# Local attention: when the next batch's first queries are turned, and in which order VectorE works around them

## The chip, the cores and the metric

The kernel is one program on one core of a Trainium2 chip. The metric is the device time of one execution in microseconds (us). A core has five engines with an instruction queue each, which run side by side and wait for each other by semaphores: TensorE (PE: matmuls, with PEld for the loading of its weights), VectorE (DVE), ScalarE (ACT), GpSimd (POOL) and SyncE (SP), which here only starts transfers. An engine does its instructions strictly in the order in which they were written.

## The reference

The program is a decoder of two layers on 16 batches of 128 tokens with 256 features: a recurrent mixer, a grouped cross attention and a mixture of experts, then local (windowed) attention, another cross attention and a gated feed-forward stage. The change touches the local attention alone:

```python
q = rms_norm(x @ Wq.T, qn_w)     # 16 heads of 128
k = rms_norm(x @ Wk.T, kn_w)     # 4 heads of 128
v = x @ Wv.T                     # 4 heads of 128
q = q * cos + rotate_half(q) * sin
k = k * cos + rotate_half(k) * sin
scores = q @ k.T / sqrt(128)     # 4 query heads share a key head
scores = where((0 <= i - j) & (i - j <= 64), scores, min)
out = softmax(scores) @ v
x = x + out @ Wo.T
```

Its input is the layer norm of x.

## The kernel before

`windowed` does the local attention. The 16 batches t follow each other (`pairs`: two written out, a loop over pairs of batches, two written out). A batch has four steps g = 0 to 3, one for each key head with its four query heads. The work is pipelined over steps: in step g of batch t each engine also does the projections and rotations that later steps need (`ahead`) and the end of the step before (`earlier`). The order on each engine is written out by hand in its own function `one`; semaphores join them. What the names mean:

- `project` (PE, L2086): six 128x512 matmuls give one group of four query heads (q0 to q3), the keys k or the values v. ACT copies the result to `wi_raw` (L2181) and squares it (L2184).
- `rotate` (DVE): the sum of squares (L2288, `wi_sums`), the cosine product (L2303, `wi_straight`) and two half-wide sine products (L2305, `wi_crossed`). `join` (POOL, L1984) adds the two; for k it also multiplies by the scale (L1987). `find_scale` (POOL, L1972 and L1973) makes the scale from the sums.
- `turn_heads` (PE, L2050): four 128x128 transposes of a joined group. `take_turned` (ACT, L2200) copies them from PSUM to `wi_q_t` or `wi_k_t`.
- `scores` (PE, L2096 the mask, L2099 the products), `maximum` (DVE, L2310, `wi_top`), `shift` (DVE, L2319, `wi_bias`), `weigh` (ACT, L2209, four exponentials), `invert` (DVE, L2332), `normalise` (POOL, L1994, `wi_weights`), `turn_weights` (PE, L2064), `take_weights` (DVE, L2326, `wi_weights_t`), `attend` (PE, L2108), `take_attended` (ACT, L2216), `split_out` (DVE, L2273), `project_out` (PE, L2121).

Below, "weights of step g" are the softmax weights. The order of PE in a step is: projections of q or k, the scores of the step, projection of v, `turn_weights` of the step before, `project_out` of two steps before, `attend` of the step before, then the transposes for the next step. At the end of step 3 these are the keys k and the queries q0 of the next batch. POOL's order in step 2 is: scale of k, `normalise` of step 2, join of k, join of q0, scale of q0; in step 3: scale of q1, `normalise` of step 3, join of q1. DVE's order over the same place, from step 2 to step 3 (L2303 to L2319):

```python
for item in items[1:]:       # step 2: q0 of the next batch
    rotate(*item)
...                          # step 3 begins
if g == 3:
    take_weights(t, 2)
maximum(t, g)
```

PE can't do the scores of step 0 before ACT has copied both turned groups, k and q0.

Of the kernel before, what the change touches and what calls it, by code (L numbers as in the profile page):

```python
# [25 lines left out]
P = 128  # L26
# [24 lines left out]
HEADS, KVH, DH = 16, 4, 128  # L51
# [1781 lines left out]
def windowed(nc, net, sem):  # L1833
# [31 lines left out]
    with ExitStack() as ctx:  # L1865
# [156 lines left out]
        def _(pe):  # L2022
# [103 lines left out]
            def one(t, s, first, last):  # L2126
                for g in range(U):
                    items = ahead(t, s, g, last)
                    for item in items:
                        if item[0] != "v":  # L2130
                            project(*item)
                    scores(t, s, g)
                    for item in items:
                        if item[0] == "v":
                            project(*item)
                    if g > 0 or not first:
                        pt, _, pg = earlier(t, s, g, 1, U)
                        turn_weights(pt, pg)
                    if g > 1 or not first:
                        pt, _, pg = earlier(t, s, g, 2, U)  # L2140
                        project_out(pt, pg)
                    if g > 0 or not first:
                        attend(*earlier(t, s, g, 1, U))
                    if g < 3:
                        turn_heads("q", t, g + 1)
                    elif not last:
                        turn_heads("k", t + 1, 0)
                        turn_heads("q", t + 1, 0)
                    if g == 0 and not last:
                        turn_h(t + 1, 1 - s)  # L2150

# [12 lines left out]
        @block.scalar  # L2164
        def _(act):
            def take(what, t, s, g):

                act.wait_ge(projected, of_six(what, t, g) + 1)
                bank = ps[:, PJ + of_six(what, 0, g) % 2, :]
                if what == "v":  # L2170
                    need(act, attended, U * (t - 1))
                    act.activation(values[:, s], bank, ACT.Copy).then_inc(proj_taken, 1)
                    return
                n, at = of_five(what, t, g), slot(what, g)

                if what == "k":
                    need(act, parts, 3 * (of_five("k", t - 1, 0) + 1))
                else:
                    need(act, parts, 3 * (of_five("q", t, g - 2) + 1) if g >= 2
                         else 3 * (of_five("q", t - 1, g + 2) + 1))  # L2180
                act.activation(raw[:, at].rearrange("p j d -> p (j d)"), bank, ACT.Copy).then_inc(proj_taken, 1)  # L2181
                act.wait_ge(proj_taken, of_six(what, t, g) + 1)
                need(act, summed, n - 1)
                act.activation(square[:, square_slot(what, t, s, g)], raw[:, at], ACT.Square).then_inc(squared, 1)  # L2184

            def take_high(name):
                act.activation(piece(w_high, name), piece(raw_w, name), ACT.Copy).then_inc(w_rounded, 1)

            def take_turned(what, t, s, g=0):
                act.wait_ge(turned, number(what, t, g) + 1)  # L2190
                bank = ps[:, bank_of(what, g), :]
                if what == "h":

                    need(act, projected, of_six("q", t - 2, 3) + 1)
                    act.activation(h_high[:, s].rearrange("p c t -> p (c t)"), bank[:, 0:D],
                                   ACT.Copy).then_inc(turned_taken, 1)
                    return
                need(act, scored, U * (t - 1) if what == "k" else U * t + g - 1)
                tile = k_t[:, s] if what == "k" else q_t[:, g % 2]
                act.activation(tile.rearrange("p j t -> p (j t)"), bank, ACT.Copy).then_inc(turned_taken, 1)  # L2200

            def weigh(t, g):

                w = U * t + g
                act.wait_ge(bias_ready, w + 1)
                need(act, turned_p, w - 1)
                need(act, inverted, w - 1)
                for j in range(4):
                    act.activation(weights[:, g % 2, j, :], ps[:, SC + g % 2, j * P:j * P + P], ACT.Exp,  # L2209
                                   bias=bias[:, g % 2, j:j + 1], scale=scale[:, g, j:j + 1],  # L2210
                                   accum_out=total[:, g % 2, j:j + 1]).then_inc(weighed, 1)

            def take_attended(t, g):
                act.wait_ge(attended, U * t + g + 1)
                need(act, output, U * t + g - 1)
                act.activation(out_high[:, g % 2].rearrange("p j t -> p (j t)"), ps[:, AV, :],  # L2216
                               ACT.Copy).then_inc(attended_taken, 1)

            def one(t, s, first, last):
                for g in range(U):  # L2220
                    for item in ahead(t, s, g, last):
                        take(*item)
                    weigh(t, g)
                    if g > 0 or not first:
                        pt, _, pg = earlier(t, s, g, 1, U)
                        take_attended(pt, pg)
                    if g < 3:
                        take_turned("q", t, s, g + 1)
                    elif not last:
                        take_turned("k", t + 1, 1 - s)  # L2230
                        take_turned("q", t + 1, 1 - s, 0)
                    if g == 0 and not last:
                        take_turned("h", t + 1, 1 - s)

            act.wait_ge(net.in_attn1, 16 * 4)
            for name in PIECES[:2]:
                take_high(name)
            take_turned("h", 0, 0)
            for name in PIECES[2:6]:
                take_high(name)  # L2240
            for item, name in zip(FIRST_ITEMS, PIECES[6:]):
                take(*item)
                take_high(name)
            take_turned("k", 0, 0)
            take_turned("q", 0, 0, 0)
            pairs(act, one)
            take_attended(NB - 1, 3)

        @block.vector
        def _(dve):  # L2250
# [26 lines left out]
            def rotate(what, t, s, g):  # L2277

                if what == "v":
                    return  # L2280
                n, at = of_five(what, t, g), slot(what, g)
                dve.wait_ge(squared, n + 1)

                if what == "k":
                    need(dve, rotated, of_five("k", t - 1, g) + 1)
                else:
                    need(dve, scaled, U * t + g - 1)
                dve.tensor_reduce(sums[:, at], square[:, square_slot(what, t, s, g)], AX.X,  # L2288
                                  ALU.add).then_inc(summed, 1)

                if what == "k":
                    need(dve, turned, number("k", t - 1) + 1)
                elif g >= 2:
                    dve.wait_ge(turned, number("q", t, g - 2) + 1)
                elif not (isinstance(t, int) and t == 0):
                    dve.wait_ge(turned, number("q", t - 1, g + 2) + 1)
                cos, sin = (tables[f"{n}_{what}"] for n in ("cos", "sin"))
                half = DH // 2

                def over_heads(table):  # L2300
                    return table.unsqueeze(1).broadcast_to([P, 4, table.shape[-1]])

                dve.tensor_tensor(straight[:, at], raw[:, at], over_heads(cos[:]), ALU.mult).then_inc(parts, 1)  # L2303
                for to, source in ((slice(0, half), slice(half, DH)), (slice(half, DH), slice(0, half))):
                    dve.tensor_tensor(crossed[:, at, :, to], raw[:, at, :, source], over_heads(sin[:, to]),  # L2305
                                      ALU.mult).then_inc(parts, 1)
# [33 lines left out]
            def one(t, s, first, last):  # L2340
                for g in range(U):
# [5 lines left out]
                    if g < 3 and (g > 0 or not first):  # L2347
                        pt, _, pg = earlier(t, s, g, 1, U)
                        take_weights(pt, pg)
                    shift(t, g)  # L2350
                    items = [item for item in ahead(t, s, g, last) if item[0] != "v"]
                    for item in items[:1]:
                        rotate(*item)
                    invert(t, g)
                    if g == 1 and not first:
                        finish(t - 1)
# [35 lines left out]
                            .broadcast_to([P, 4, P])).then_inc(tables_ready, 1)  # L2392
            for item in FIRST_ITEMS:
                rotate(*item)
            for name in LOW_BY_DVE[4:]:
                take_low(dve, name, low_dve)
            pairs(dve, one)
# [692 lines left out]
```

## Time and profile before

| | |
|---|---|
| median of 3 runs | 1493.51 us (1492.75 to 1494.72) |
| time of the profiled execution | 1493.66 us |
| its span | 1491.6 us |
| PE busy | 1249.2 us (84% of the span) |
| PEld busy | 983.0 us (66%) |
| DVE busy | 981.7 us (66%) |
| ACT busy | 843.0 us (57%) |
| POOL busy | 641.1 us (43%) |
| mean granted clock of PE | 0.936 of full speed |

The span is the time from the first to the last instruction; the 2.06 us by which the time of the same execution is longer lie around it. Busy shares are means over six stages with different limits. The local attention takes the stretch from about 660 to 1135 us of the span.

### The profile page before, as it was taken

How to read it: one execution, taken by the hardware profiler on the slowest of the kernel's cores; microseconds unless marked ns; L12 is line 12 of the kernel's file. 1: busy time of each engine (PE TensorE's matmuls, PEld its weight loads, DVE VectorE, ACT ScalarE, POOL GpSimd, SP SyncE). 2: the span in 40 equal slices, each digit the busy share in tenths (PEclk: the TensorE clock that was granted, in tenths of full speed). 3: DMA queues.
4: the chain of work that ended last, by engine and by line, in shares of the span. 5: the costliest groups of instructions: out<-in, count | busy, mean ns of one | idle time of the engine just before them, and what ended most of it. 6: DMA issues, size and time to landing. Idle time of an engine off the chain costs nothing. (4 is left out here: it accounts for less than half of the span.)

```text
span 1491.6 us, 26479 instructions
## 1 busy us (share of the span) xinstructions
PE 1249.2 (84%) x7839; PEld 983.0 (66%) x7886; DVE 981.7 (66%) x1905; ACT 843.0 (57%) x2174; POOL 641.1 (43%) x724
## 2 busy tenths in 40 slices
PE   6994889995793999638998998899896888879998
PEld 4673555554683897526777777777774555548887
DVE  5998788883453544797778778777773566643443
ACT  5443899993452555545666666666662555543322
POOL 2003666663436015457667666666663333320000
PEclk9996999997797999958999999999998999988999
DMA  8400433310003454120000000000000000000000
GB/s 312 156 0 14 105 93 84 84 43 1 0 33 116 142 195 138 29 102 1 2 1 0 0 0 0 0 0 0 0 1 3 4 4 3 3 1 1 15 14 29
DMA packets 49684, 64.52 MB, mean 43 GB/s; under 512 B 6032, under 2 KB 42896, under 8 KB 48336
## 3 DMA queue, kind: packets, MB, share of 16 engines
q1 hardware_dynamic: 46544, 55.27, 11.8%
q0 software_dynamic: 3072, 8.39, 1.7%
q8 instruction: 37, 0.61, 0.2%
q14 instruction: 31, 0.25, 0.1%
HBM read 38.48 MB, written 16.78 MB: 37 GB/s over the span
## 5 line engine op out<-in xcount | busy, mean ns | idle before, releaser
L2209 ACT ACTIVATE wi_weights<-wi_psum,wi_bias,wi_scale 128x128 f32<-128x128 f32 x256 | 113.7, 454 | 118.2 <-DVE wi_bias L2319 118.2
L929 ACT ACTIVATE gq_weights<-gq_psum,gq_least 128x128 f32<-128x128 f32 x512 | 151.2, 524 | 2.0 <-DVE gq_least L977 2.0
L1984 POOL TENSOR_TENSOR wi_straight<-wi_straight,wi_crossed 128x512 f32<-128x512 f32 x80 | 103.3, 1291 | 10.9 <-DVE wi_crossed L2305 10.8
L977 DVE TENSOR_REDUCE gq_least<-gq_psum 128x4 f32<-128x512 f32 x128 | 86.1, 686 | 26.9 <-PE gq_psum L854 25.5
L1972 POOL TENSOR_TENSOR wi_scratch<-wi_sums,wi_eps 128x4 f32<-128x4 f32 x80 | 35.1, 438 | 132.6 <-DVE wi_sums L2288 131.2
L1973 POOL TENSOR_TENSOR wi_scale<-wi_scratch,minus_half 128x4 f32<-128x4 f32 x80 | 84.6, 1058 | 6.3
L2108 PE MATMUL wi_psum<-wi_weights_t,wi_values 128*128 128x512 f32 x128 | 68.9, 620 | 20.6 <-DVE wi_weights_t L2326 20.6
L2310 DVE TENSOR_REDUCE wi_top<-wi_psum 128x4 f32<-128x512 f32 x64 | 44.0, 687 | 63.1 <-PE wi_psum L2099 63.1
L2099 PE MATMUL wi_psum<-wi_k_t,wi_q_t 128*128 128x128 f32 x512 | 67.5, 275 | 19.8 <-ACT wi_q_t L2200 18.7
L862 PE MATMUL gq_psum<-const,gq_weights 128*128 128x128 f32 x512 | 79.1, 278 | 1.3 <-ACT gq_weights_t L937 0.3
L2735 DVE TENSOR_REDUCE cr_top<-cr_psum 128x4 f32<-128x512 f32 x64 | 43.7, 682 | 46.0 <-PE cr_psum L2550 46.0
L862 PEld LDWEIGHTS gq_psum<-const,gq_weights 128*128 128x128 f32 x512 | 63.1, 142 | 14.8 <-DVE gq_weights_t L990 4.2
L1994 POOL TENSOR_TENSOR wi_weights<-wi_weights,wi_inverse 128x512 f32<-128x512 f32 x64 | 66.2, 1034 | 9.5 <-remote 5.1
L2099 PEld LDWEIGHTS wi_psum<-wi_k_t,wi_q_t 128*128 128x128 f32 x512 | 67.9, 193 | 1.6
L2050 PEld LDWEIGHTS wi_psum<-const,wi_straight 128*128 128x128 f32 x320 | 39.6, 143 | 42.7 <-issue 41.8
L2490 POOL TENSOR_TENSOR cr_keys_diagonal<-cr_qk,const 128x256 f32<-128x256 f32 x32 | 19.4, 626 | 112.0 <-ACT cr_qk L2662 112.0
L854 PE MATMUL gq_psum<-gq_keys_diagonal,gq_h_t 128*128 128x512 f32 x128 | 63.8, 503 | 3.7 <-ACT gq_weights L929 3.7
L2305 DVE TENSOR_TENSOR wi_crossed<-wi_raw,wi_sin_q 128x256 f32<-128x256 f32 x128 | 64.9, 547 | 0.0
L2303 DVE TENSOR_TENSOR wi_straight<-wi_raw,wi_cos_q 128x512 f32<-128x512 f32 x64 | 61.0, 953 | 0.0
L2928 DVE TENSOR_TENSOR ff_gated<-ff_gated,ff_psum 128x512 f32<-128x512 f32 x32 | 22.0, 688 | 58.3 <-PE ff_psum L2848 58.0
L2181 ACT ACTIVATE wi_raw<-wi_psum 128x512 f32<-128x512 f32 x80 | 48.3, 603 | 20.7 <-PE wi_psum L2086 20.2
L2326 DVE COPY wi_weights_t<-wi_psum 128x512 f32<-128x512 f32 x64 | 43.8, 684 | 21.8 <-PE wi_psum L2064 21.6
(384 smaller groups left out, 3890.0 us busy)
## 6 DMA issues: line engine op xcount, KB each, us to landing
gq_keys<-in_ctx_keys_dram SPq DMA_DIRECT2D x16, 512.0 KB, 3.8
gq_keys_diagonal<-gq_key_parts SPq DMA_DIRECT2D x64, 128.0 KB, 3.9
slot_x<-rw_zero SPq DMA_DIRECT2D x1, 5120.0 KB, 18.0
ex_slot_rows<-slot_x SPq DMA_DIRECT2D x20, 256.0 KB, 3.0
slot_y<-ex_s_out SPq DMA_DIRECT2D x20, 256.0 KB, 2.2
x<-in_x_dram SPq DMA_DIRECT2D x4, 512.0 KB, 8.8
gate<-in_gate_dram SPq DMA_DIRECT2D x2, 1024.0 KB, 5.3
up<-in_up_dram SPq DMA_DIRECT2D x2, 1024.0 KB, 7.5
```

What stands on the lines that cost most here:

```text
L854: pe.matmul(ps[:, u % 4, :], h_t[:, s, u, :], kbd[s][:, u, :, :], start=True, stop=True).then_inc(scored, 1)
L862: mm = pe.transpose(ps[:, bank(unit, t, u), j * P:j * P + P], weights[:, u % RINGS, j * P:j * P + P], ident)
L929: e = act.activation(weights[:, u % RINGS, j * P:j * P + P], ps[:, u % 4, j * P:j * P + P], ACT.Exp, bias=least[:, u % 4, j:j + 1], scale= ...
L977: dve.tensor_reduce(least[:, u % 4, :], rows(u), AX.X, ALU.min).then_inc(topped, 1)
L1973: found = pool.tensor_tensor(scale[:, scale_at], scratch2[:], net.half[:, 0:4], ALU.pow)
L1984: added_up = pool.tensor_tensor(straight[:, at], straight[:, at], crossed[:, at], ALU.add)
L1994: pool.tensor_tensor(weights[:, g % 2], weights[:, g % 2], wide(inverse[:, g % 2], [P, 4, P]), ALU.mult).then_inc(normalised, 1)
L2099: mm = pe.matmul(bank[:, j * P:j * P + P], q_t[:, g % 2, j, :], k_t[:, s, g, :], start=False, stop=(j == 3), skip_group_check=True)
L2108: pe.matmul(ps[:, AV, :], values[:, s, g * DH:g * DH + DH], weights_t[:, g % 2], start=True, stop=True).then_inc(attended, 1)
L2209: act.activation(weights[:, g % 2, j, :], ps[:, SC + g % 2, j * P:j * P + P], ACT.Exp, bias=bias[:, g % 2, j:j + 1], scale=scale[:, g, j:j ...
L2303: dve.tensor_tensor(straight[:, at], raw[:, at], over_heads(cos[:]), ALU.mult).then_inc(parts, 1)
L2305: dve.tensor_tensor(crossed[:, at, :, to], raw[:, at, :, source], over_heads(sin[:, to]), ALU.mult).then_inc(parts, 1)
```

## The change

Two orders are changed, and no instruction is added or removed.

First, `turn_heads` of q0 moves on PE from the end of step 3 of a batch to step 0 of the next, behind the projection of q2 and ahead of the scores. ACT's copy of q0 moves with it, to the head of step 0.

Second, `rotate` is cut in two: it keeps the sum of squares and the cosine product, and `rotate_crossed` does the two sine products. Everywhere `rotate_crossed` follows `rotate` at once, except for q0 of the next batch: its sine products are done in step 3, behind `take_weights` of step 2, `maximum` and `shift` of step 3.

```diff
@@ PE, one
                     for item in items:
                         if item[0] != "v":
                             project(*item)
+                    if g == 0 and not first:
+                        turn_heads("q", t, 0)
                     scores(t, s, g)
...
                         turn_heads("q", t, g + 1)
                     elif not last:
                         turn_heads("k", t + 1, 0)
-                        turn_heads("q", t + 1, 0)
@@ ACT, one
                 for g in range(U):
+                    if g == 0 and not first:
+                        take_turned("q", t, s, 0)
                     for item in ahead(t, s, g, last):
                         take(*item)
...
                     elif not last:
                         take_turned("k", t + 1, 1 - s)
-                        take_turned("q", t + 1, 1 - s, 0)
@@ DVE, rotate and one
-                cos, sin = (tables[f"{n}_{what}"] for n in ("cos", "sin"))
-                half = DH // 2
+                cos = tables[f"cos_{what}"]
...
                 dve.tensor_tensor(straight[:, at], raw[:, at], over_heads(cos[:]), ALU.mult).then_inc(parts, 1)
+
+            def rotate_crossed(what, t, s, g):
...
+                n, at = of_five(what, t, g), slot(what, g)
+                sin, half = tables[f"sin_{what}"], DH // 2
...
                 for to, source in ((slice(0, half), slice(half, DH)), (slice(half, DH), slice(0, half))):
                     dve.tensor_tensor(crossed[:, at, :, to], raw[:, at, :, source], over_heads(sin[:, to]),
                                       ALU.mult).then_inc(parts, 1)
...
                     shift(t, g)
+                    if g == 3 and not last:
+                        rotate_crossed("q", t + 1, 1 - s, 0)
                     items = [item for item in ahead(t, s, g, last) if item[0] != "v"]
                     for item in items[:1]:
                         rotate(*item)
+                        rotate_crossed(*item)
                     invert(t, g)
```

PE before, from `attend` of step 2 (L2108) in step 3 to the scores of step 0 of the next batch (L2099), inside the loop:

```order
L2108 MATMUL wi_psum<-wi_weights_t,wi_values 128x512
L2035 ISA
L2050 MATMUL wi_psum<-const,wi_straight 128x128 x4
L2035 REGISTER_ALU
L2050 MATMUL wi_psum<-const,wi_straight 128x128 x4
L88 REGISTER_ALU
L2086 MATMUL wi_psum<-wi_wq_high,wi_h_high 128x512 x2
L2086 MATMUL wi_psum<-wi_wq_low,wi_h_high 128x512 x2
L2086 MATMUL wi_psum<-wi_wq_high,wi_h_low 128x512 x2
L88 ISA
L2096 MATMUL wi_psum<-wi_mask,wi_ident 128x512
L2099 MATMUL wi_psum<-wi_k_t,wi_q_t 128x128 x4
```

PE of the changed kernel, same place:

```order
L2108 MATMUL wi_psum<-wi_weights_t,wi_values 128x512
L2035 ISA
L2050 MATMUL wi_psum<-const,wi_straight 128x128 x4
L88 REGISTER_ALU
L2086 MATMUL wi_psum<-wi_wq_high,wi_h_high 128x512 x2
L2086 MATMUL wi_psum<-wi_wq_low,wi_h_high 128x512 x2
L2086 MATMUL wi_psum<-wi_wq_high,wi_h_low 128x512 x2
L2035 REGISTER_ALU
L2050 MATMUL wi_psum<-const,wi_straight 128x128 x4
L88 ISA
L2096 MATMUL wi_psum<-wi_mask,wi_ident 128x512
L2099 MATMUL wi_psum<-wi_k_t,wi_q_t 128x128 x4
```

The second group of four transposes (q0) has moved past the six matmuls of the projection of q2, and now stands directly ahead of the mask and the scores.

DVE before, from the cosine product of q0 (L2303) at the end of step 2 to the reciprocal of step 3 (L2332):

```order
L2303 TENSOR_TENSOR wi_straight<-wi_raw,wi_cos_q 128x512
L2305 TENSOR_TENSOR wi_crossed<-wi_raw,wi_sin_q 128x4x64 x2
L2326 COPY wi_weights_t<-wi_psum 128x512
L2309 REGISTER_ALU
L2310 TENSOR_REDUCE wi_top<-wi_psum 128x4
L2319 SCALAR_TENSOR_TENSOR wi_bias<-wi_top,wi_scale 128x4
L2282 REGISTER_ALU
L2288 TENSOR_REDUCE wi_sums<-wi_square 128x4
L2296 REGISTER_ALU
L2303 TENSOR_TENSOR wi_straight<-wi_raw,wi_cos_q 128x512
L2305 TENSOR_TENSOR wi_crossed<-wi_raw,wi_sin_q 128x4x64 x2
L2330 REGISTER_ALU
```

DVE of the changed kernel, same place (its lines are numbered anew: L2303 is L2304, L2305 is L2317, L2326 is L2338, L2310 is L2322, L2319 is L2331, L2288 is L2290):

```order
L2304 TENSOR_TENSOR wi_straight<-wi_raw,wi_cos_q 128x512
L2338 COPY wi_weights_t<-wi_psum 128x512
L2321 REGISTER_ALU
L2322 TENSOR_REDUCE wi_top<-wi_psum 128x4
L2331 SCALAR_TENSOR_TENSOR wi_bias<-wi_top,wi_scale 128x4
L2317 TENSOR_TENSOR wi_crossed<-wi_raw,wi_sin_q 128x4x64 x2
L2284 REGISTER_ALU
L2290 TENSOR_REDUCE wi_sums<-wi_square 128x4
L2298 REGISTER_ALU
L2304 TENSOR_TENSOR wi_straight<-wi_raw,wi_cos_q 128x512
L2317 TENSOR_TENSOR wi_crossed<-wi_raw,wi_sin_q 128x4x64 x2
L2342 REGISTER_ALU
```

The sine products of q0 have moved behind the copy of the weights, the maximum and the bias. POOL's order is the same in both kernels.

## Rows read from the trace of the kernel before

**Rows 1.** Windows: length, busy us (count) of PE, PEld, DVE, ACT, POOL; clock; DMA.

```profile
857.60:886.40 28.80, 26.25 (x167) 21.64 (x168) 22.22 (x44) 18.76 (x54) 19.04 (x20) 1.00 0.00 0
...
1132.00:1136.00 4.00, 3.82 (x14) 2.46 (x12) 0.67 (x1) 0.15 (x1) 0.00 (x0) 0.57 0.02 4
```

**Rows 2.** Waits in the stage: us in total, times, longest.

```profile
PE wi_psum L2108 <- DVE wi_weights_t L2326: 20.6, 16, 1.3
...
PE wi_psum L2099 <- ACT wi_q_t L2200: 18.7, 16, 1.4
```

**Rows 3.** Timeline, one boundary: start, us, engine, what [idle before].

```profile
869.42 1.27 POOL L1984 TENSOR_TENSOR wi_straight<-wi_straight,wi_crossed 128x512 f32<-128x512 f32 x1
869.57 1.67 DVE L2303 TENSOR_TENSOR wi_straight<-wi_raw,wi_cos_q 128x512 f32<-128x512 f32 x1
...
870.77 1.37 POOL L1987 TENSOR_TENSOR wi_straight<-wi_straight,wi_scale 128x512 f32<-128x512 f32 x1
...
871.16 1.59 DVE L2305 TENSOR_TENSOR wi_crossed<-wi_raw,wi_sin_q 128x256 f32<-128x256 f32 x2
...
872.68 0.68 DVE L2326 COPY wi_weights_t<-wi_psum 128x512 f32<-128x512 f32 x1
872.84 1.26 POOL L1984 TENSOR_TENSOR wi_straight<-wi_straight,wi_crossed 128x512 f32<-128x512 f32 x1 [0.70 <-DVE wi_crossed L2305]
873.28 0.67 DVE L2310 TENSOR_REDUCE wi_top<-wi_psum 128x4 f32<-128x512 f32 x1
...
873.41 1.13 PE L2108 MATMUL wi_psum<-wi_weights_t,wi_values 128*128 128x512 f32 x2 [1.31 <-DVE wi_weights_t L2326]
...
873.99 0.16 DVE L2319 SCALAR_TENSOR_TENSOR wi_bias<-wi_top,wi_scale 128x4 f32<-128x4 f32 x1
874.06 0.20 POOL L1972 TENSOR_TENSOR wi_scratch<-wi_sums,wi_eps 128x4 f32<-128x4 f32 x1
874.15 0.69 DVE L2288 TENSOR_REDUCE wi_sums<-wi_square 128x4 f32<-128x512 f32 x1
...
874.34 1.01 POOL L1973 TENSOR_TENSOR wi_scale<-wi_scratch,minus_half 128x4 f32<-128x4 f32 x1
...
875.36 0.75 DVE L2305 TENSOR_TENSOR wi_crossed<-wi_raw,wi_sin_q 128x256 f32<-128x256 f32 x2
...
875.42 0.41 POOL L1972 TENSOR_TENSOR wi_scratch<-wi_sums,wi_eps 128x4 f32<-128x4 f32 x1
...
875.91 1.06 POOL L1973 TENSOR_TENSOR wi_scale<-wi_scratch,minus_half 128x4 f32<-128x4 f32 x1
...
876.89 0.62 ACT L2200 ACTIVATE wi_q_t<-wi_psum 128x512 f32<-128x512 f32 x1
876.95 1.03 POOL L1994 TENSOR_TENSOR wi_weights<-wi_weights,wi_inverse 128x512 f32<-128x512 f32 x1
...
877.98 1.05 PE L2099 MATMUL wi_psum<-wi_k_t,wi_q_t 128*128 128x128 f32 x8 [1.17 <-ACT wi_q_t L2200]
...
879.23 0.72 PE L2121 MATMUL wi_psum<-wi_wo_high,wi_out_high 128*128 128x256 f32 x4
...
902.08 0.67 DVE L2310 TENSOR_REDUCE wi_top<-wi_psum 128x4 f32<-128x512 f32 x1
```

**Rows 4.** Timeline at the start of the stage: a join and a waiting cosine product.

```profile
666.41 1.26 POOL L1984 TENSOR_TENSOR wi_straight<-wi_straight,wi_crossed 128x512 f32<-128x512 f32 x1 [0.36 <-DVE wi_crossed L2305]
666.86 1.37 DVE L2303 TENSOR_TENSOR wi_straight<-wi_raw,wi_cos_q 128x512 f32<-128x512 f32 x1
...
667.64 0.65 POOL L1972 TENSOR_TENSOR wi_scratch<-wi_sums,wi_eps 128x4 f32<-128x4 f32 x1
...
668.37 1.07 POOL L1973 TENSOR_TENSOR wi_scale<-wi_scratch,minus_half 128x4 f32<-128x4 f32 x1
```

**Rows 5.** Timeline at the end of the stage: PE waits for POOL's weights.

```profile
1130.19 1.04 POOL L1994 TENSOR_TENSOR wi_weights<-wi_weights,wi_inverse 128x512 f32<-128x512 f32 x1 [5.13 <-remote]
...
1131.70 0.92 PE L2121 MATMUL wi_psum<-wi_wo_high,wi_out_high 128*128 128x256 f32 x4
```

More of the change, by code:

```diff
@@ L2303, in rotate, with over_heads @@
                 dve.tensor_tensor(straight[:, at], raw[:, at], over_heads(cos[:]), ALU.mult).then_inc(parts, 1)
+            def rotate_crossed(what, t, s, g):
+                if what == "v":
+                    return
+                n, at = of_five(what, t, g), slot(what, g)
+                sin, half = tables[f"sin_{what}"], DH // 2
+                def over_heads(table):
+                    return table.unsqueeze(1).broadcast_to([P, 4, table.shape[-1]])
                 for to, source in ((slice(0, half), slice(half, DH)), (slice(half, DH), slice(0, half))):
@@ L2394, in _ @@
                 rotate(*item)
+                rotate_crossed(*item)
             for name in LOW_BY_DVE[4:]:
```

## The prediction

> **What bounds the kernel now.** I read the windows over the attention stage first, then its list of waits, then the timeline of one boundary between two batches, and last two odd places of the timeline that show what the boundary does not. In the windows one batch takes 28.80 us, PE is busy 26.25 of them at a granted clock of 1.00, and no other engine comes above 22.22 [rows 1]. The maxima of step 3 of two successive batches start at 873.28 and 902.08, so the period is 28.80 us too [rows 3]. PE is thus the pace-maker, and a change can gain only what PE waits. The list of waits shows two PE waits that come once a batch: 20.6 us in 16 times before `attend` and 18.7 us in 16 times before the scores [rows 2]. In the timeline they are the 1.31 us ahead of 873.41, released by the copy of the weights, and the 1.17 us ahead of 877.98, released by ACT's copy of q0 [rows 3]. Both lie at the boundary from step 3 of a batch to step 0 of the next. There are 15 boundaries. Elsewhere PE goes from one instruction to the next, and all others follow it.
>
> The reader is to see why these waits exist. At 869.57 DVE begins the cosine product of q0 while POOL joins k (869.42 to 870.69); it ends only at 871.24, 0.55 behind the end of the join. The sine products then stand behind POOL's next instruction (870.77 to 872.14) and end at 872.75 [rows 3]. Where no join or product of POOL is in their way the two take 0.75 (875.36) [rows 3]. Only then come the copy of the weights (872.68), the maximum (873.28) and the bias (873.99). So DVE's product and POOL's join exclude each other; the copy and the maximum do not mind POOL's join of q0 at 872.84, they take 0.68 and 0.67 beside it [rows 3].
>
> **The change, part by part.** I work in the time frame of rows 3. Up to the cosine product of q0 nothing changes, since everything there follows PE.
>
> DVE, step 3. The copy of the weights starts where the sine products did, at 871.16. The maximum follows 0.60 later (873.28 - 872.68), at 871.76, and the bias 0.71 after it (873.99 - 873.28), at 872.47. The bias is 1.52 us earlier. The sine products of q0 come behind it. The order shows no register instruction between them, so I take the usual overlap: next start 0.08 ahead of the end (871.16 against 871.24), that is 872.47 + 0.16 - 0.08 = 872.55; as upper end the 0.16 that the sum of squares stood behind the bias (874.15 - 873.99), 872.63. POOL has been idle since 872.14, so they take 0.75 and end at 873.30 to 873.38. Before they ended at 872.75: the ready time of q0's parts moves **later by 0.55 to 0.63 us**.
>
> PE's first wait. The copied weights are there at 871.16 + 0.68 = 871.84, while PE itself is free only at 873.41 - 1.31 = 872.10. The wait of 1.31 us goes, and `attend`, the transposes of k and the projection of q2 run 1.31 us earlier.
>
> PE's second wait. Without both waits PE would be at the scores of step 0 at 877.98 - 1.31 - 1.17 = 875.50. But now the transposes of q0 stand right ahead of them, and the projection of q2 no longer hides ACT's copy. That copy takes 0.62, and the products start 0.47 after its end (877.51 to 877.98); I take 1.1 us for the new wait. The join of q0 ends at about 874.7, before its transposes. So the scores of step 0 start at about 876.6, 1.4 us earlier than before.
>
> POOL, where the gain is lost. Behind the scores PE transposes the weights of step 3, and these come from POOL's `normalise`. POOL's queue at this place is join of q0, scale of q0 (two instructions), scale of q1 (two), `normalise` of step 3. None of them waits for another engine before: from 872.84 to 876.95 + 1.03 = 877.98 it is one chain of 5.14 us [rows 3]. Its head waits for the sine products that the change puts back. The join starts 0.09 behind them (872.84 - 872.75): at 873.39 to 873.47.
>
> The chain also gets longer. DVE's sum of squares of q1 starts at about 873.23 and its cosine product at about 873.85, inside the join of q0 that lasts until 874.65. The start of the stage shows the same meeting: join at 666.41, cosine product at 666.86 held until 668.23, POOL's addition behind the join stretched to 0.65, and the power at 668.37, 1.96 us after the join's start [rows 4]. At the boundary before it was 874.34 - 872.84 = 1.50. That is +0.46. The power then takes 1.07 and not 1.01, +0.06. The second addition (875.42, 0.41) finds DVE's sine products done and takes 0.20, -0.21; the second power takes 1.01 to 1.06, 0 to -0.05. Chain: 5.14 + 0.46 + 0.06 - 0.21 = 5.45, or 5.40. The weights of step 3 are ready at 873.39 + 5.40 = 878.79 to 873.47 + 5.45 = 878.92, where it was 877.98.
>
> The Trainium skill's page SBUF — State Buffer (section "SBUF: two separate sides") has a rule that speaks against this change: VectorE's second read port is GpSimd's own, whoever begins first holds it for the whole instruction and the other fully blocks. By that rule the price of the new meeting would be just the DVE work left behind the join, 0.55; the rows give 0.46 and the sum goes by them.
>
> Sum. At the end of the stage PE waits for `normalise`: it ends at 1130.19 + 1.04 = 1131.23 and `project_out` starts at 1131.70, 0.47 later [rows 5]. At the boundary `project_out` started at 879.23 [rows 3]; now it starts at 878.79 + 0.47 = 879.26 to 878.92 + 0.47 = 879.39. From there PE runs without a wait as before. The period changes by **+0.03 to +0.16 us**; I take +0.06, near the lower end, because the 0.08 behind the bias fits the order better. Fifteen boundaries give +0.9 us (+0.5 to +2.4). The moved copy on ACT and the cut of `rotate` into two cost nothing: the exponentials start 1.5 us earlier, so ACT has room at the boundary, and DVE's instructions are the same in number. If that cover went, the copy of q2 behind that of q0 would be late by 0.62 us, still ahead of the bias of step 0. The sum is made on the profiled execution, 1493.66, which is 0.15 above the median of three: 1493.66 + 0.9 - 0.15 = 1494.4.
>
> **The rivals.** *The full gain (A).* The two parts do what they seem to do: PE keeps the 1.4 us of the scores at each boundary, 15 x 1.4 = 21 us, 1473. It needs the weights of step 3 at 877.5, and POOL's chain, measured at 5.14 us without a gap, would have to start at 872.4, before the sine products have even begun. Only if POOL's durations here hide waits that would shrink could part of this come.
>
> *POOL goes first (B).* The pair of q1's cosine product and POOL's additions may go the other way: POOL, whose addition is sent 0.03 ahead of its join's end (667.64 against 667.67), takes its turn before DVE does. Then the first addition takes 0.20 and the chain is about 5.00 us; the weights are ready at 878.39, PE goes on at 878.86, 0.37 earlier, 15 x 0.37 = 5.6 us, 1488. Against it: rows 4, and in rows 3 the cosine product of q0 came in between POOL's join of k and its product of k.
>
> *The clock falls (C), the slower side.* PE now has two waits with only the mask and the scores between them: 1.1 us behind q0's transposes, and about 1.3 us (from 877.5 to 878.8) before the weights of step 3. Before they were 1.31 and 1.17 with two groups of work between, at a clock of 1.00 [rows 1, 3]. At the end of the stage, behind a longer wait, a window of 4 us had 0.57, between the levels of 1.2 and 2.4 GHz, with 3.82 us of PE work [rows 1]. That work at full clock is about 3.82 x 0.57 = 2.2, so 1.6 us lost. It decides as soon as the clock of the boundary falls once a batch: 15 x 1.6 = 24 us, 1518. The Trainium skill's TensorE: Matmul & The Clock Gate ("HAM oscillation — how this bites in real kernels") describes just that, a loop whose every turn waits and starts again at half rate; no boundary of this trace shows it.
>
> *A longer slip (D).* The same chain as forecast, but with restarts of PE and POOL dearer than the rows say, over 0.2 us a boundary: 1497 to 1499.
>
> **How the numbers follow.** A measurement of this kernel can tell about 0.2% from no change, 3.0 us, which is 0.2 us a boundary. The forecast mechanism (POOL's chain sets the boundary) has 0.73: within 0.2 us 0.60, beyond it on the slow side (D) 0.13. B 0.11, A 0.05, C 0.06; 0.05 is left for what I don't see, split 0.02 faster and 0.03 slower. Faster: 0.11 + 0.05 + 0.02 = 0.18. Slower: 0.13 + 0.06 + 0.03 = 0.22. Same 0.60. The range takes in B's 1488 and D's 1499, and leaves A and C out.
>
> **What would show it.** In the changed trace: the wait of 1.31 us before `attend` gone; the bias of step 3 about 1.5 us earlier; POOL's join of q0 0.55 to 0.63 later, its first addition behind it stretched to about 0.65; a new wait of PE's `turn_weights` for `wi_weights` of POOL, 15 times over 1 us; the period 28.8 to 29.0. I would be wrong if PE's `turn_weights` at the boundary did not wait for POOL, if POOL's chain took clearly less than 5.4 us, or if the clock of a mid-stage window fell below 1.00.

## The result: 1.0034 times as long, 95% interval 1.0026 to 1.0042

The changed kernel takes 1499.07 us (median of 12 runs, 1494.88 to 1501.57); the kernel before, run beside it, 1493.92 us (12 runs, 1491.81 to 1494.72). It is slower by 5.1 us. The runs of the changed kernel are spread over 6.7 us, those of before over 2.9; measured again in the experiments below it is 4.7 against 5.9, so only the shift of the median came twice, not the wider spread.

The page of the changed kernel, its head and two groups that answer to what the prediction spoke of (POOL's joins and PE's transposes of the weights; busy us, mean ns, then idle time before them with its releaser):

```profile
span 1498.9 us, 26520 instructions
...
L1984 POOL TENSOR_TENSOR wi_straight<-wi_straight,wi_crossed 128x512 f32<-128x512 f32 x80 | 103.3, 1291 | 19.1 <-DVE wi_crossed L2317 19.1
...
L2064 PE MATMUL wi_psum<-const,wi_weights 128*128 128x128 f32 x256 | 41.3, 286 | 21.7 <-POOL wi_weights L1994 21.7
```

The list of waits of the stage in the changed kernel:

```profile
PE wi_psum L2064 <- POOL wi_weights L1994: 21.7, 16, 2.5
...
PE wi_psum L2096 <- ACT wi_q_t L2201: 19.3, 18, 3.3
...
PE wi_psum L2108 <- DVE wi_weights_t L2338: 0.8, 1, 0.8
```

The wait before `attend`, 20.6 us in [rows 2], is down to 0.8. In its place stands one of 21.7 us for POOL's weights. The wait for ACT's copy of q0 is a little smaller (it is now counted at the mask, L2096, the first instruction behind it, and 3.3 of the 19.3 us are one wait at the start of the stage).

The timeline of one boundary of the changed kernel, between the same two batches as [rows 3]:

```profile
870.78 1.68 DVE L2304 TENSOR_TENSOR wi_straight<-wi_raw,wi_cos_q 128x512 f32<-128x512 f32 x1
...
872.38 0.68 DVE L2338 COPY wi_weights_t<-wi_psum 128x512 f32<-128x512 f32 x1
...
872.98 0.67 DVE L2322 TENSOR_REDUCE wi_top<-wi_psum 128x4 f32<-128x512 f32 x1
...
873.69 0.16 DVE L2331 SCALAR_TENSOR_TENSOR wi_bias<-wi_top,wi_scale 128x4 f32<-128x4 f32 x1
873.77 0.75 DVE L2317 TENSOR_TENSOR wi_crossed<-wi_raw,wi_sin_q 128x256 f32<-128x256 f32 x2
...
874.60 1.30 POOL L1984 TENSOR_TENSOR wi_straight<-wi_straight,wi_crossed 128x512 f32<-128x512 f32 x1 [1.25 <-DVE wi_crossed L2317]
...
875.03 1.42 DVE L2304 TENSOR_TENSOR wi_straight<-wi_raw,wi_cos_q 128x512 f32<-128x512 f32 x1
...
875.85 0.66 POOL L1972 TENSOR_TENSOR wi_scratch<-wi_sums,wi_eps 128x4 f32<-128x4 f32 x1
...
876.59 1.07 POOL L1973 TENSOR_TENSOR wi_scale<-wi_scratch,minus_half 128x4 f32<-128x4 f32 x1
...
877.57 0.39 PE L2096 MATMUL wi_psum<-wi_mask,wi_ident 128*128 128x512 bf16 x1 [0.96 <-ACT wi_q_t L2201]
...
878.99 1.04 POOL L1994 TENSOR_TENSOR wi_weights<-wi_weights,wi_inverse 128x512 f32<-128x512 f32 x1
...
880.08 1.11 PE L2064 MATMUL wi_psum<-const,wi_weights 128*128 128x128 f32 x4 [1.24 <-POOL wi_weights L1994]
```

From the cosine product of q0 to the bias it is 2.91 us (873.69 - 870.78), where [rows 3] have 4.42: 1.51 earlier. From there on the reader sees POOL's chain: join at 874.60, weights ready at 880.03. PE has waited since 878.8. And its transposes of the weights, four of them, take 1.11 us, where 0.60 to 0.66 is usual: the clock has fallen, as the windows below show.

The maxima of step 3 in four successive batches (`wi_top`, changed kernel) give the period:

```profile
844.13 0.67 DVE L2322 TENSOR_REDUCE wi_top<-wi_psum 128x4 f32<-128x512 f32 x1
...
872.98 0.67 DVE L2322 TENSOR_REDUCE wi_top<-wi_psum 128x4 f32<-128x512 f32 x1
...
903.21 0.67 DVE L2322 TENSOR_REDUCE wi_top<-wi_psum 128x4 f32<-128x512 f32 x1
...
933.60 0.67 DVE L2322 TENSOR_REDUCE wi_top<-wi_psum 128x4 f32<-128x512 f32 x1
```

The first distance is 28.85 us, and so are most others in this stage (the first two are 29.08 and 29.15). The next two are 30.23 and 30.39. Windows over the same place (length, busy us of PE, PEld, DVE, ACT, POOL, then PE's granted clock as a share of full speed, DMA) show why:

```profile
878.00:880.00 2.00, 0.85 (x8) 0.65 (x6) 0.80 (x2) 0.47 (x1) 1.99 (x3) 0.94 0.00 0
880.00:882.00 2.00, 1.92 (x9) 1.92 (x10) 0.77 (x3) 0.00 (x0) 1.25 (x2) 0.50 0.00 0
882.00:884.00 2.00, 2.00 (x11) 1.73 (x10) 1.93 (x5) 1.87 (x8) 1.17 (x2) 0.70 0.00 0
850.00:879.00 29.00, 26.74 (x167) 21.65 (x166) 21.50 (x45) 18.87 (x53) 19.42 (x22) 1.00 0.00 0
879.00:908.00 29.00, 26.95 (x158) 22.09 (x159) 20.92 (x44) 18.23 (x52) 18.13 (x20) 0.94 0.00 0
```

Right behind the two waits the granted clock is 0.50 (1.2 GHz); in the window from 882 to 884 it is 0.70, so it comes back to 1.00 (2.4 GHz) there, within 4 us. This happened at 4 of the 15 boundaries of the profiled execution: the periods 30.23, 30.39 and 30.20, and the last boundary, where 26.89 us pass from the maximum of step 3 to the last maximum of the stage, against 25.35 in the kernel with both waits filled, below. Together 1.38 + 1.54 + 1.35 + 1.54 = 5.8 us.

The span is 7.3 us longer than before, so 1.5 us are not from the low clock. They lie in this stage too. To see them, take the time from the maximum of step 2 of the first batch to the `normalise` of step 3 of the last. First the changed kernel, then a version of it in which PE's second wait is filled with work (described below), last the kernel before, whose `normalise` at 1130.19 is in [rows 5]:

```profile
692.18 0.69 DVE L2322 TENSOR_REDUCE wi_top<-wi_psum 128x4 f32<-128x512 f32 x1 [2.37 <-PE wi_psum L2099]
...
1137.99 1.04 POOL L1994 TENSOR_TENSOR wi_weights<-wi_weights,wi_inverse 128x512 f32<-128x512 f32 x1 [5.13 <-remote]
```

```profile
690.70 0.69 DVE L2330 TENSOR_REDUCE wi_top<-wi_psum 128x4 f32<-128x512 f32 x1 [3.99 <-PE wi_psum L2107]
...
1130.75 1.04 POOL L1994 TENSOR_TENSOR wi_weights<-wi_weights,wi_inverse 128x512 f32<-128x512 f32 x1 [5.13 <-remote]
```

```profile
691.71 0.69 DVE L2310 TENSOR_REDUCE wi_top<-wi_psum 128x4 f32<-128x512 f32 x1 [4.02 <-PE wi_psum L2099]
```

It is 445.81 us in the changed kernel, 440.05 with the wait filled and 438.48 before. So the changed order costs the stage 1.6 us where no clock falls, and the falls cost the other 5.8.

### The profile page after: what moved, and what is told of

The parts are those of the page before. It is cut to its first block and busy times, and to the rows that moved or that the text cites. A ratio compares the mean times of both kernels' runs of the same rounds, so it can differ in the third digit from the quotient of the medians.

```text
span 1498.9 us, 26520 instructions
## 1 busy us (share of the span) xinstructions
PE 1265.0 (84%) x7886; PEld 989.2 (66%) x7886; DVE 969.9 (65%) x1905; ACT 844.5 (56%) x2174; POOL 644.9 (43%) x724
## 5 line engine op out<-in xcount | busy, mean ns | idle before, releaser
L1972 POOL TENSOR_TENSOR wi_scratch<-wi_sums,wi_eps 128x4 f32<-128x4 f32 x80 | 39.8, 497 | 125.1 <-DVE wi_sums L2290 123.8
L2322 DVE TENSOR_REDUCE wi_top<-wi_psum 128x4 f32<-128x512 f32 x64 | 44.0, 687 | 62.5 <-PE wi_psum L2099 62.5
L2304 DVE TENSOR_TENSOR wi_straight<-wi_raw,wi_cos_q 128x512 f32<-128x512 f32 x64 | 71.8, 1123 | 0.0
L2338 DVE COPY wi_weights_t<-wi_psum 128x512 f32<-128x512 f32 x64 | 43.9, 685 | 43.0 <-PE wi_psum L2064 43.0
L2099 PEld LDWEIGHTS wi_psum<-wi_k_t,wi_q_t 128*128 128x128 f32 x512 | 68.5, 194 | 1.7
L2099 PE MATMUL wi_psum<-wi_k_t,wi_q_t 128*128 128x128 f32 x512 | 68.1, 276 | 0.0
L2506 POOL TENSOR_TENSOR cr_keys_diagonal<-cr_qk,const 128x256 f32<-128x256 f32 x32 | 19.3, 626 | 113.3 <-ACT cr_qk L2678 113.3
L2108 PE MATMUL wi_psum<-wi_weights_t,wi_values 128*128 128x512 f32 x128 | 66.9, 603 | 0.8 <-DVE wi_weights_t L2338 0.8
L2064 PE MATMUL wi_psum<-const,wi_weights 128*128 128x128 f32 x256 | 41.3, 286 | 21.7 <-POOL wi_weights L1994 21.7
```

The costliest lines, as they stand in the source:

```text
L2099: mm = pe.matmul(bank[:, j * P:j * P + P], q_t[:, g % 2, j, :], k_t[:, s, g, :], start=False, stop=(j == 3), skip_group_check=True)
L2108: pe.matmul(ps[:, AV, :], values[:, s, g * DH:g * DH + DH], weights_t[:, g % 2], start=True, stop=True).then_inc(attended, 1)
```

## The experiments

Each kernel was run against the kernel before on the same chip. The ratios are to the kernel before as it ran in the same round, so they need not follow from the medians of two rounds; the batch is the distance of two maxima of step 3 in mid-stage.

| kernel | median us | ratio (95%) | batch us |
|---|---|---|---|
| changed kernel, again | 1499.03 | 1.0028 (1.0019 to 1.0038) | 28.85, three of 30.2 to 30.4 |
| transposes moved alone | 1492.37 | 0.9995 (0.9986 to 1.0003) | 28.80 |
| sine products moved alone | 1494.19 | 1.0006 (0.9996 to 1.0016) | 28.82 |
| changed, both waits filled | 1494.21 | 0.9998 (0.9987 to 1.0008) | 28.85 |
| changed, second wait filled | 1492.95 | 0.9996 (0.9987 to 1.0005) | 28.85 |
| changed, first wait filled | 1494.36 | 1.0000 (0.9991 to 1.0010) | 28.84 |
| changed, `normalise` ahead of both scales | 1490.99 | 0.9983 (0.9971 to 0.9996) | 28.64 to 28.79 |
| changed, POOL reordered | 1479.05 | 0.9902 (0.9887 to 0.9917) | 27.85 |
| sine products and POOL's order | 1480.00 | 0.9907 (0.9892 to 0.9922) | 27.83 to 27.95 |
| POOL's order alone | 1492.91 | 1.0001 (0.9993 to 1.0010) | 28.80 |
| transposes and POOL's order | 1493.65 | 1.0003 (0.9994 to 1.0012) | 28.80 |

**One part at a time.** The transposes alone, that is without this:

```diff
-                    if g == 3 and not last:
-                        rotate_crossed("q", t + 1, 1 - s, 0)
...
                     for item in items[1:]:
                         rotate(*item)
+                        rotate_crossed(*item)
```

> Only the transposes of q0 are moved; VectorE keeps the order of before. Theory (POOL's chain sets the boundary, and what is on top comes from TensorE's clock falling at some boundaries): POOL's weights of step 3 are ready as early as before, PE still waits 1.3 us before attend, and the scores start about when they did, so the period stays at 28.7 to 28.8, the clock stays at 1.00 in the mid-stage windows, 1492 to 1494.5. Rival (the move of the transposes itself costs, because PE now waits for ACT's copy right ahead of the scores): the period is 28.9 to 29.2 and the time 1496 to 1500.

The sine products alone, with `turn_heads` and `take_turned` of q0 at the end of step 3:

```diff
-                    if g == 0 and not first:
-                        turn_heads("q", t, 0)
...
                         turn_heads("k", t + 1, 0)
+                        turn_heads("q", t + 1, 0)
... (the two lines of take_turned on ACT likewise)
```

> Only the sine products of q0 are moved; PE turns q0 at the end of step 3 as before. Theory: the join of q0 ends 0.55 us later, PE waits for it about 1.5 us before the transposes of q0, and again about 1 us for POOL's weights of step 3; the period is 28.85 as with both parts, since the same POOL chain sets it. The waits have the projection of q2 between them, so the clock falls seldom: 1494 to 1496. Rival (the falls of the clock come with any longer wait at the boundary): 1498 to 1502 with windows under 1.00. Rival (the period is set by PE's order): clearly over 28.9 in every batch.

Neither part alone slows the kernel by more than these runs can tell. The waits of PE in the first, then in the second:

```profile
PE wi_psum L2108 <- DVE wi_weights_t L2338: 20.6, 16, 1.3
PE wi_psum L2099 <- ACT wi_q_t L2201: 18.7, 16, 1.4
```

```profile
PE wi_psum L2050 <- POOL wi_straight L1984: 19.2, 16, 1.2
PE wi_psum L2064 <- POOL wi_weights L1994: 17.1, 16, 2.5
```

With the transposes moved alone both old waits are there to the tenth of a us: ACT's own queue (exponentials, two copies, then q0's) sets the scores of step 0, not the place of the transposes. With the sine products alone PE waits for the joined q0 and for the weights of step 3; the projection of q2 lies between the two, and the clock is 1.00 in mid-stage. The period is the 28.8 us of POOL's chain. Both expectations held, though PE's wait for the joined q0 is 1.2 us and not 1.5.

**Filling the waits.** The changed kernel with four mask matmuls in each wait; their result is overwritten by the scores that follow, and the added `wait_ge` lets them begin only when ACT has read the scores that stood in that place before:

```diff
+            def fill(bank, count):
+                for _ in range(count):
+                    pe.matmul(ps[:, SC + bank, :], ident_b[:], mask.rearrange("p j t -> p (j t)"), start=True,
+                              stop=True, skip_group_check=True)
...
             def scores(t, s, g):
+                if g == 0 and not (isinstance(t, int) and t == 0):
+                    pe.wait_ge(weighed, 4 * (U * t - 1))
+                    fill(0, 4)
...
             def turn_weights(t, g):
+                if g == 3 and not (isinstance(t, int) and t == NB - 1):
+                    pe.wait_ge(weighed, 4 * U * (t + 1))
+                    fill(1, 4)
```

> The changed kernel with four more matmuls of the mask (bf16, 128x512, results overwritten) in each of PE's two waits at the boundary: ahead of the scores of step 0 and ahead of turn_weights of step 3. Theory: PE is not idle in the waits, so the clock stays at 1.00 at all boundaries, every batch takes 28.85 to 28.95, and the time is 1494 to 1496 with a small spread over the runs. Rival (the 5 us are longer restarts and not the clock, or the clock falls for another reason): 1498 to 1501 with the spread of the changed kernel.

The 5 us are gone, with eight matmuls a boundary more, and no boundary of the profiled execution is over 28.86 in mid-stage. The small spread that I expected did not come: the runs reach from 1491.50 to 1497.42, and the profiled one takes 1497.18 without a single slow boundary. What varies there lies outside these boundaries. The changed kernel itself, again, as control, and only one of the two waits filled:

> The changed kernel once more, as it is, as the control for the other kernels of this round. Theory: 1497 to 1500, with a spread of several us from run to run, since the number of boundaries at which the clock falls differs; every fall costs 1.4 to 1.5 us. Rival (the first measurement was a chance result): 1493 to 1495.

> The changed kernel with four overwritten matmuls of the mask only in the second wait, ahead of turn_weights of step 3; the wait for ACT's copy of q0 stays empty. Theory (it takes both waits close together for the clock to fall): one filled wait is enough, no batch over 28.9, 1494 to 1496. Rival (the wait ahead of the scores does it alone): falls stay, 1497 to 1500.

> The changed kernel with the four overwritten matmuls of the mask only in the first wait, ahead of the scores of step 0; the wait for POOL's weights of step 3 stays empty at about 1.2 us. Theory (the clock falls when both waits are empty, with little work between): no batch over 28.9, 1493 to 1495.5. Rival (the wait for the weights of step 3 is enough by itself): falls of 1.4 to 1.5 us stay at some boundaries, 1497 to 1500.

The control gives the same 5 us, and its profiled execution has the low clock at the same boundaries as the first (30.27, 30.39, 30.21 and the last, 26.90). Filling either wait removes them all in the profiled executions, and the medians are 4.7 and 6.1 us under that of the control. The kernel with the second wait filled is 1 us faster than I expected. With only the second filled, PE at the boundary and two mid-stage windows:

```profile
876.12 0.39 PE L2104 MATMUL wi_psum<-wi_mask,wi_ident 128*128 128x512 bf16 x1 [0.96 <-ACT wi_q_t L2209]
876.34 1.05 PE L2107 MATMUL wi_psum<-wi_k_t,wi_q_t 128*128 128x128 f32 x8
877.23 1.03 PE L2095 MATMUL wi_psum<-wi_mask,wi_ident 128*128 128x512 bf16 x4
878.63 0.66 PE L2067 MATMUL wi_psum<-const,wi_weights 128*128 128x128 f32 x4 [0.38 <-POOL wi_weights L1994]
```

```profile
850.05:878.90 28.85, 27.52 (x172) 21.96 (x171) 21.38 (x44) 18.89 (x53) 19.28 (x21) 1.00 0.00 0
878.90:907.75 28.85, 27.60 (x172) 21.95 (x171) 21.38 (x44) 18.89 (x53) 19.29 (x21) 1.00 0.00 0
```

With only the first filled the second stays whole, and still nothing is lost:

```profile
874.80 1.03 PE L2092 MATMUL wi_psum<-wi_mask,wi_ident 128*128 128x512 bf16 x4
...
878.43 0.66 PE L2064 MATMUL wi_psum<-const,wi_weights 128*128 128x128 f32 x4 [1.39 <-POOL wi_weights L1994]
```

So it is not either wait, but both empty with only the mask and the scores between them. The wait for POOL by itself brings no low clock: the period is 28.84 with it. The rivals of these expectations (a first result by chance; longer restarts; one of the waits enough alone) are out.

But the filled kernels differ from the changed one at a second place, too. At the end of the stage, where nothing is filled, PE waits 2.51 us for the last weights in all of them. From the start of the last `normalise` to that of the last matmuls of `project_out`, in the kernel before and with the second wait filled:

```profile
1130.19:1138.35 8.16, 5.56 (x27) 4.23 (x28) 2.08 (x3) 0.80 (x2) 1.04 (x1) 0.79 0.01 2
```

```profile
1130.75:1137.33 6.58, 3.98 (x27) 3.18 (x27) 2.08 (x3) 0.80 (x2) 1.04 (x1) 1.00 0.00 0
```

The same 27 matmuls take 1.6 us less, at a clock of 1.00 and not 0.79. All three kernels with a filled wait show this (6.57 to 6.58 us), and none of the ten others does (7.9 to 8.2 us, the changed kernel 8.11). So their ratios of 0.9996 to 1.0000 hold two things: 1.5 to 1.6 us lost in the batches and 1.6 us won at the end. Why filling a wait some 20 us earlier keeps the clock up there is open.

**Taking away POOL's chain.** In the changed kernel, `normalise` of step 3 directly behind the join of q0, both scales behind it:

```diff
+                    if g == 3:
+                        normalise(t, g)
+                        if not last:
+                            find_scale("q", t + 1, 1 - s, 0)
                     for item in items[:1]:
                         find_scale(*item)
-                    normalise(t, g)
+                    if g < 3:
+                        normalise(t, g)
...
                     for item in items[1:]:
                         join(*item)
-                        find_scale(*item)
```

> The changed kernel with POOL's order in step 3 altered: normalise of step 3 directly behind the join of q0, the two scales of q0 and q1 behind it. Theory: the weights of step 3 no longer stand behind four instructions of 2.4 us, PE's wait for them goes, and the boundary keeps what the change freed on PE: about 1.4 us at each of 15 boundaries, 1471 to 1477, clock at 1.00. Rival (DVE or ACT bind next at the same place, POOL was only the last to be seen): 1487 to 1495.

The expected 20 us did not come, only 2.4 (its interval ends at 0.9996). The number is the rival's, and its cause in part. The wait for the weights is gone, but POOL's join of q1 is now late, as POOL's timeline and the list of PE's waits show: `normalise` itself now waits 1.39 us for DVE's reciprocal, and both scales stand between it and the join.

```profile
933.28 1.04 POOL L1994 TENSOR_TENSOR wi_weights<-wi_weights,wi_inverse 128x512 f32<-128x512 f32 x1 [1.39 <-DVE wi_inverse L2348]
934.27 0.25 POOL L1972 TENSOR_TENSOR wi_scratch<-wi_sums,wi_eps 128x4 f32<-128x4 f32 x1
934.60 1.01 POOL L1973 TENSOR_TENSOR wi_scale<-wi_scratch,minus_half 128x4 f32<-128x4 f32 x1
935.69 0.20 POOL L1972 TENSOR_TENSOR wi_scratch<-wi_sums,wi_eps 128x4 f32<-128x4 f32 x1
935.97 1.01 POOL L1973 TENSOR_TENSOR wi_scale<-wi_scratch,minus_half 128x4 f32<-128x4 f32 x1
936.95 1.60 POOL L1984 TENSOR_TENSOR wi_straight<-wi_straight,wi_crossed 128x512 f32<-128x512 f32 x1
```

```profile
PE wi_psum L2103 <- ACT wi_q_t L2205: 18.5, 16, 1.4
PE wi_psum L2054 <- POOL wi_straight L1984: 15.8, 16, 1.1
```

So the next version has the join between the scales:

```diff
+                    if g == 3:
+                        normalise(t, g)
+                        if not last:
+                            find_scale("q", t + 1, 1 - s, 0)
+                            join("q", t + 1, 1 - s, 1)
+                            find_scale("q", t + 1, 1 - s, 1)
+                        continue
...
                     for item in items[1:]:
                         join(*item)
-                        find_scale(*item)
```

> The changed kernel with POOL's order in step 3: join of q0, normalise of step 3, scale of q0, join of q1, scale of q1. With both scales ahead of the join of q1, PE waited 1.03 us for that join before the transposes of q1 in step 0. Theory: now neither the weights of step 3 nor the joined q1 are late, PE loses only the wait for the copy of q0, and a batch takes 27.5 to 27.8 us: 1475 to 1480. Rival (DVE's products of q2 collide with the join of q1 in the same way, or ACT binds): 28.6 and 1489 to 1492.

1479.05 us, 1% under the kernel before (4 runs): the best version of this study. A batch takes 27.85, a little over the 27.5 to 27.8 that I expected. The same order of POOL with each part of the change alone, and with neither:

> The same POOL order, with the moved sine products, but the transposes of q0 at the end of step 3 as in the kernel before. Theory: PE waits about 1.5 us for the join of q0 instead of 1.0 for ACT's copy behind the projection, so a batch takes 0.4 to 0.6 us longer than with both parts: 28.0 to 28.3, 1483 to 1488. Rival (the move of the transposes is worth nothing): the same time as with both parts.

> The kernel before with POOL's order alone altered (join of q0, normalise of step 3, scale of q0, join of q1, scale of q1). Theory: before the change POOL's weights of step 3 were ready 0.8 us before PE came to them, so an earlier normalise is worth nothing; the batch stays at 28.8 and the time at 1492 to 1494.5. Rival (POOL's order is worth its 14 us or a part of it without the moved sine products): 1479 to 1490.

> Moved transposes and POOL's new order, with VectorE as in the kernel before. Theory: the bias of step 3 is as late as before, ACT's exponentials and copies behind it set the scores of step 0, so this too stays at 28.8 and 1492 to 1494.5. Rival (the transposes and POOL together free the boundary without the sine products): 1479 to 1490.

The gain of 14 us needs two things and no third: the moved sine products and POOL's order. POOL's order alone is worth nothing (it removed a wait that was not there), the sine products alone nothing (they ran into POOL). The moved transposes add nothing in any pair: with them 1479.05 and 27.85 a batch, without 1480.00 and 27.83 to 27.95. The 0.4 to 0.6 us a batch that I expected of them were wrong. With them the scores of step 0 do come 0.2 us earlier behind those of step 3 (7.40 to 7.49 against 7.63 to 7.74), but those of step 1 come 0.2 later behind step 0 (6.26 to 6.35 against 6.08 to 6.12).

## Why the prediction was right, and where it was not

Its range (1488.0 to 1499.5) holds the time, 0.4 us under the upper end, but its likeliest case, no change at 1494.4, is not what was measured. That the range holds it is luck: the upper end was drawn for rival D, dearer restarts, which did not happen. What made the kernel slower is mostly rival C, the clock, which the range leaves out (5.8 of the 7.3 us of the profiled execution). Of the three signs of being wrong one came true: a mid-stage window fell to a clock of 0.94.

*The waits and the bias.* Right. The bias comes 1.51 earlier (1.52 said), the wait of 1.31 us is gone, and the new wait ahead of the scores is 0.96 us (1.1 said).

*Ready time of q0's parts.* Right. The sine products start 0.08 behind the bias (873.77 - 873.69), the lower of the two ends that I gave, and the one that I took.

*POOL's chain.* Right to 0.03 us. From the join's start to the ready weights it is 880.03 - 874.60 = 5.43 (5.40 to 5.45 said). The cosine product of q1 was held for 1.42, POOL's first addition stretched to 0.66 and the power came 1.99 behind the join's start (1.96 said). DVE went first where POOL's addition waited too, so rival B is out. The Trainium skill's rule that the prediction named (SBUF — State Buffer, "SBUF: two separate sides"), the full block, agrees with these rows.

*The period.* +0.05 us (28.85 against 28.80) in mid-stage where +0.06 was taken. But at the first two boundaries and the last two the kernel with its second wait filled loses 0.43, 0.15, 0.19 and 0.29 against before (between maxima of step 2), so all fifteen cost 1.6 us and not 0.9, inside the +0.5 to +2.4. This is the forecast mechanism without the low clock. The ratios of the filled kernels, 1.0000, 0.9996 and 0.9998, look better than that because of the 1.6 us at the end of the stage.

*The clock.* Here the prediction failed. Rival C had the right place (the boundary), the right cause (two waits with only the mask and the scores between) and nearly the right price (1.6 us; measured 1.35 to 1.54 at a boundary, and 1.6 at the end of the stage, where it was read). Wrong was the step "it decides as soon as the clock of the boundary falls once a batch: 15 x 1.6": I took it as all or nothing, so that the case was 24 us or 0 and got 0.06. What happened lies between, 4 boundaries of 15 in the profiled executions. Both profiled executions, 1500.94 and 1500.11 us, are among the slowest of their kernel. From the medians it is (1499.07 - 1493.92 - 1.6) / 1.45 = 2 to 3 boundaries, an estimate that takes off the 1.6 us of the order. The Trainium skill's rule that the prediction cited (TensorE: Matmul & The Clock Gate, "HAM oscillation — how this bites in real kernels"), that each turn of such a loop starts again at half rate, agrees in kind with the rows and not in number. The slower side had 0.22; most of it on D, dearer restarts, which did not happen: the period without a low clock is right.

*Full gain (A).* Rightly excluded for the change as it stands. Its price, 1.4 us a boundary and 1473, was right for the place it was worked out for and too high for the batch. In the changed kernel and in the best version the scores of step 0 start 7.4 to 7.5 us behind those of step 3 of the batch before, where it was 8.8: the 1.4 are there, with the wait of 0.96 us for ACT's copy already taken off. But in the best version the scores of step 1 come 6.26 to 6.35 behind those of step 0, where it was 5.90, and that takes 0.4 back, so 1.0 us a batch and 14 us in all are left. The rows of one boundary show the place: PE waits again, for ACT's copy of q1.

```profile
875.65 0.61 ACT L2207 ACTIVATE wi_q_t<-wi_psum 128x512 f32<-128x512 f32 x1
...
876.39 0.39 PE L2102 MATMUL wi_psum<-wi_mask,wi_ident 128*128 128x512 bf16 x1 [0.30 <-ACT wi_q_t L2207]
```

ACT goes from the bias of step 0 to this copy without a gap, and that bias took 0.67 us longer than usual, beside POOL's join of q1 (the rows are in the last section). With the new order of POOL and the moved sine products alone the bias is held less, it takes 0.36 to 0.56 us in mid-stage, and the scores of step 1 are 0.2 earlier. That this delay is the 0.4 is argued from these rows; no kernel was run without it.

## What to carry to other kernels

Where a piece of work on one engine moves back to let something pass, ask who waits for the piece and what is queued behind that one: here 1.5 us won on VectorE at each boundary were lost in GpSimd's queue, and two thirds of that got back by another order of six instructions there. When a change lets waits draw together on TensorE, look for what work is left between them, and price a lower clock for a few of the turns, not for all or none. A few matmuls whose result is thrown away in one of the waits told whether the clock was the cause. But look in their trace for other places where the clock changed with them, here 1.6 us at the end of the stage.

## What the runs showed of the hardware

All boundaries of the changed kernel are alike, and yet the clock fell to 0.50 only at some, the same ones in two profiled executions (batches 6 to 7, 7 to 8, 13 to 14 and the last). Why these is open. Over the 12 runs the time goes with the mean clock, 1494.88 us at 0.938 and 1501.57 at 0.931, but that alone does not point at these boundaries: with the sine products moved alone there are runs of 1491.65 us at 0.940 and 1498.19 at 0.933, and its profiled execution has no slow boundary.

Whether the clock falls is not settled by the wait next to it alone. At the end of the stage PE waits 2.51 us in the kernel before, in the changed one and in that with the second wait filled; the clock falls behind it in the first two and stays at 1.00 in the third, whose last filled wait lies some 20 us back.

A tiny VectorE instruction can be held by a GpSimd one as a large one is. In the best version the bias of step 0, 4 elements from two inputs in SBUF, falls into a join at every boundary and takes 0.44 to 1.05 us, where it is 0.15 in the kernel before. At this one it took 0.82 and ended 0.03 behind the join:

```profile
872.07 1.28 POOL L1984 TENSOR_TENSOR wi_straight<-wi_straight,wi_crossed 128x512 f32<-128x512 f32 x1
```

```profile
872.56 0.82 DVE L2337 SCALAR_TENSOR_TENSOR wi_bias<-wi_top,wi_scale 128x4 f32<-128x4 f32 x1
```
